# Graph network on one core: gather slots, index loads and table order of the attention edges

## What is computed

```python
def gatv2_layer(x, src, dst, Wl, bl, Wr, br, att, bias, n_nodes):
    C = att.shape[1]
    xl = (x @ Wl + bl).reshape(n_nodes, H, C)
    xr = (x @ Wr + br).reshape(n_nodes, H, C)
    e = jax.nn.leaky_relu(xl[src] + xr[dst], NEG_SLOPE)
    alpha = jnp.einsum('ehc,hc->eh', e, att)
    ...
    return out.mean(axis=1) + bias
```

## Time and profile before

| | us |
|---|---|
| median of 3 runs | 8165.79 (8153.4 to 8166.29) |
| the profiled execution's own time | 8135.08 |
| its span | 8133.5 |

### The profile page before, as it was taken

One profiled execution on the slowest core, in us unless ns is written; L12 is line 12 of the kernel. 1 busy time (PEld: TensorE's weight loads), 2 busy tenths in 40 slices (PEclk: granted clock), 3 DMA queues, 4 the chain that ended last, 5 costly groups with the idle time before them and its releaser, 6 DMA issues. The chain is left out here.

```text
span 8133.5 us, 102622 instructions
## 1 busy us (share of the span) xinstructions
PE 3894.0 (48%) x24731; PEld 3130.5 (38%) x24802; DVE 5407.7 (66%) x9588; ACT 2288.6 (28%) x3006; POOL 3503.5 (43%) x3810
## 2 busy tenths in 40 slices
PE   5777774000488826665362222223776222222476
PEld 2777773000388825565330000002763000001375
DVE  6777776968211146667437888885874888887686
ACT  5555553127122226566311111110001111111000
POOL 4766662001100067777515666661001666665100
PEclk9555555555699967877655555556975555555796
DMA  8899898955488723333336666663634666665462
GB/s 312 253 270 274 266 273 240 246 222 202 96 290 290 275 92 114 122 134 134 67 91 189 189 189 188 188 186 79 125 90 136 188 189 188 189 188 144 107 126 58
DMA packets 1551059, 1463.90 MB, mean 180 GB/s; under 512 B 1295757, under 2 KB 1343529, under 8 KB 1534460
## 3 DMA queue, kind: packets, MB, share of 16 engines
q1 hardware_dynamic: 976448, 824.48, 32.6%
q0 software_dynamic: 175712, 462.09, 20.9%
q10 hardware_dynamic: 398812, 176.37, 8.0%
HBM read 1080.92 MB, written 381.40 MB: 180 GB/s over the span
## 5 line engine op out<-in xcount | busy, mean ns | idle before, releaser
L2320 POOL DMA_INDIRECT rows_p<-node_rows,stage_i x1728 | 1638.0, 948 | 596.9 <-issue 482.7
L2356 PE MATMUL psZ<-parts_r,hot_t 126*128 x1728 | 629.6, 468 | 1859.8 <-DVE lz L2423 1720.0
L2356 PEld LDWEIGHTS psZ<-parts_r,hot_t 126*128 126x128 bf16 x1728 | 180.5, 104 | 2309.8 <-issue 2289.2
L2416 DVE TENSOR_TENSOR psZ<-psZ,rows_p 128x660 f32<-128x660 f32 x864 | 725.4, 847 | 476.1 <-DMA rows_p<-node_rows,stage_i 404.7
L257 POOL DMA_INDIRECT rows_s<-hpx,stage_i x784 | 740.5, 945 | 264.7 <-issue 240.7
L257 POOL DMA_INDIRECT both<-table,stage_i x784 | 740.5, 944 | 263.9 <-issue 239.7
L715 PE MATMUL psP<-window,pair_hot 128*128 x3136 | 715.8, 423 | 263.1 <-DVE pair_run L790 178.3
L715 PEld LDWEIGHTS psP<-window,pair_hot 128*128 128x128 f32 x3136 | 686.6, 331 | 295.8 <-issue 295.8
L2385 ACT ACTIVATE near<-locs,third 126x1536 bf16<-126x1536 bf16 x144 | 226.8, 1575 | 1923.4 <-DMA locs<-loc_rows 1923.3
L2423 DVE SCALAR_TENSOR_TENSOR lz<-psZ,att 128x660 f32<-128x660 f32 x864 | 722.9, 837 | 2.5
L2429 DVE TENSOR_REDUCE sc<-lz 128x10 f32<-128x660 f32 x864 | 711.8, 831 | 0.0
(11 more groups left out here) (523 smaller groups left out, 7527.7 us busy)
## 6 DMA issues: line engine op xcount, KB each, us to landing
tile<-adj SPq DMA_DIRECT2D x228, 781.2 KB, 4.6
xs<-x_src SPq DMA_DIRECT2D x648, 128.0 KB
x_src<-rows_p SPq DMA_DIRECT2D x144, 384.0 KB, 3.6
locs<-loc_rows SPq DMA_DIRECT2D x144, 378.0 KB
hpx<-stage ACTq DMA_DIRECT2D x25, 2048.0 KB, 7.5
pair_loc<-pair_locs SPq DMA_DIRECT2D x28, 1792.0 KB, 11.1
window<-hpx SPq DMA_DIRECT2D x196, 256.0 KB
dst_runs<-pair_run SPq DMA_DIRECT2D x28, 1792.0 KB
```

The costliest lines, as they stand in the source:

```text
L2320: pool.indirect_dma_start(rows[:, k, j, :], None, g.node_rows, bass.IndirectOffsetOnAxis(stage[:, k, j:j + 1], 0)).then_inc(got[k], 16)
L2356: last = pe.matmul(psZ[:, n % 4, j, 0:ZH], hot[:, k, col * CE:(col + 1) * CE], parts[:, bass.ds(at[col], 1), :].rearrange("p o c -> p (o c)"),
L2416: v.tensor_tensor(here, here, rows[:, k, m * G:(m + 1) * G, 0:ZH], ALU.add).then_inc(added, 1)
```

## The change

One function changes, `gat_edges`, in three ways.
- The ring of gathered rows has four slots of KS = 6 columns in place of two of twelve, with a semaphore of each kind per slot. The memory is the same. DVE waits for a slot at every third group (GS = 3) and marks it used there.
- POOL no longer copies indices. SP loads them from `srcT` into `stage`, a slot of six at a time: four loads ahead of the table stage, and one as soon as a slot's gathers have landed, ahead of the slot's store.
- The table stage does one source block and one target block per iteration, 25 times. The sum of both products is made by DVE (one more step) and not by PE. `parts` is loaded by one DMA from SP.

```diff
-    XK = (NB + 3) // 2
+    SLOTS = 4
+    KS = 2 * KC // SLOTS
+    GS = KS // G
     with phase(nc) as s:
-        stage = s.sb("stage_i", [P, 2, KC], i32)
+        stage = s.sb("stage_i", [P, SLOTS, KS], i32)
...
             def _(sp):
                 sp.dma_start(g.node_rows.rearrange("(p b) c -> p b c", b=NB)[:, :, ZH:TR], h[:, :, :]).then_inc(put, 16)
+                for k in range(SLOTS):
+                    sp.dma_start(stage[:, k, :], g.srcT[:, k * KS:(k + 1) * KS]).then_inc(index_in[k], 16)
...
-                def store(i, k):
-                    sp.wait_ge(got[k], i * (16 * KC) + 16 * KC)
-                    sp.dma_start(g.x_src.rearrange("(j p) c -> p j c", p=P)[:, bass.ds((i * 2 + k) * KC, KC), :],
+                def load_index(i, k):
+                    at = bass.ds(i * (SLOTS * KS) + k * KS, KS)
+                    sp.dma_start(stage[:, k, :], g.srcT[:, at]).then_inc(index_in[k], 16)
+
+                def store(i, k, last):
+                    sp.wait_ge(got[k], i * (16 * KS) + 16 * KS)
+                    if not last:
+                        load_index(i + 1, k)
+                    sp.dma_start(g.x_src.rearrange("(j p) c -> p j c", p=P)[:, bass.ds(i * (SLOTS * KS) + k * KS, KS), :],
                                  rows[:, k, :, ZH:TR]).then_inc(stored[k], 16)
...
                 with sp.Fori(0, NK // 2 - 1) as i:
                     load_locs(i, 1)
-                    store(i, 0)
+                    store(i, 0, False)
+                    store(i, 1, False)
                     load_locs(i + 1, 0)
-                    store(i, 1)
+                    store(i, 2, False)
+                    store(i, 3, False)
...
                 with pool.Fori(0, NK // 2) as i:
-                    c.begin(i, 2)
-                    for k in range(2):
-
+                    for k in range(SLOTS):
+                        pool.wait_ge(index_in[k], i * 16 + 16)
                         pool.wait_ge(used[k], i + 1)
                         pool.wait_ge(stored[k], i * 16 + 16)
-                        c.link(pool.tensor_copy(stage[:, k, :], g.srcT[:, bass.ds((i * 2 + k) * KC, KC)]))
                         pool.sem_inc(staged, 1)
-                        for j in range(KC):
+                        for j in range(KS):
...
+                    pe.transpose(psZ[0:D, 3, b % 2, 0:P], h[:, b, :], g.ident[:, :]).then_inc(n_turned, 1)
+                    pe.wait_ge(n_ready, b + 1)
...
+                    pe.matmul(psZ[:, 0, b % 2, 0:ZH], xT[:, b % 2, :], flat(g.wA[:, :, :]), start=True, stop=True)
+                    pe.matmul(psZ[:, 1, b % 2, 0:ZH], xT[:, b % 2, :], flat(g.wB[:, :, :]), start=True, stop=True).then_inc(n_made, 1)
...
-                    c.link(v.scalar_tensor_tensor(zs, psZ[:, 2, b % 2, 0:ZH], 0.0, att, ALU.max, ALU.mult))
+                    c.link(v.tensor_tensor(zs, tab[:, b % 2, :], psZ[:, 1, b % 2, 0:ZH], ALU.add))
                     c.mark(v.tensor_copy(x3[:, b % 2, 1, :], rest))
+                    c.link(v.scalar_tensor_tensor(zs, zs, 0.0, att, ALU.max, ALU.mult))
+                    c.mark(v.tensor_tensor(x3[:, b % 2, 2, :], rest, x3[:, b % 2, 1, :], ALU.subtract))
                     c.link(v.tensor_reduce(selfs[:, b, :], zs.rearrange("p (h c) -> p h c", h=H), X, ALU.add))
-                    c.link(v.tensor_tensor(x3[:, b % 2, 2, :], rest, x3[:, b % 2, 1, :], ALU.subtract))
...
-                            if m == 0:
-                                v.wait_ge(got[k], i * (16 * KC) + 16 * KC)
+                            slot, at = divmod(n, GS)
+                            if at == 0:
+                                v.wait_ge(got[slot], i * (16 * KS) + 16 * KS)
...
-                            if q % NG == NG - 1:
-                                v.sem_inc(used[q // NG], 1)
+                            if q % GS == GS - 1:
+                                v.sem_inc(used[q // GS], 1)
```

More of the change, by code:

```diff
@@ L2242, in gat_edges @@
         tab = s.sb("tab_rows", [P, 2, ZH])
-        xT, x3 = s.sb("xT", [D + 1, XK, P]), s.sb("x3", [P, 2, 3, ZH], bf16)
+        xT, x3 = s.sb("xT", [D + 1, 2, P]), s.sb("x3", [P, 2, 3, ZH], bf16)
         psZ = s.ps("psZ", [P, 4, G, 512])
         two = lambda name: [s.sem(f"{name}{k}") for k in range(2)]
[L2247 to L2250, removed]
+        locs_in, sent, tab_put = (two(n) for n in ("locs_in", "sent", "tab_put"))
+        slots = lambda name: [s.sem(f"{name}{k}") for k in range(SLOTS)]
+        used, stored, index_in = (slots(n) for n in ("slot_used", "stored", "index_in"))
+        got = [s.pool_sem(g, k) for k in range(SLOTS)]
+        dve_c, staged, put, parts_in, cleared = (
+            s.sem(n) for n in ("dve_c", "staged", "x_put", "parts_in", "cleared"))
         hot_made, made, added, prod, scored, neared = (s.sem(n) for n in ("hot_made", "made", "added", "prod", "scored", "neared"))
-        padded, n_turned, n_ready, n_made, n_tab, n_both, n_high, n_split = (
-            s.sem(n) for n in ("padded", "n_turned", "n_ready", "n_made", "n_tab", "n_both", "n_high", "n_split"))
-        sources = lambda b: range(2 * b, min(2 * b + 2, NB))
+        padded, n_turned, n_ready, n_made, n_tab, n_high, n_split = (
+            s.sem(n) for n in ("padded", "n_turned", "n_ready", "n_made", "n_tab", "n_high", "n_split"))
         grp = lambda i, n: i * (2 * NG) + (n + 1)
@@ L2292, in _ @@
                     load_locs(i, 1)
-                    store(i, 0)
+                    store(i, 0, False)
+                    store(i, 1, False)
                     load_locs(i + 1, 0)
-                    store(i, 1)
+                    store(i, 2, False)
+                    store(i, 3, False)
                 load_locs(NK // 2 - 1, 1)
-                store(NK // 2 - 1, 0)
-                store(NK // 2 - 1, 1)
-                for k in range(2):
+                for k in range(SLOTS):
+                    store(NK // 2 - 1, k, True)
+                for k in range(SLOTS):
                     sp.wait_ge(stored[k], 16 * (NK // 2) + 16)
@@ L2303, in _ @@
             def _(pool):
-                c = Chain(pool, pool_c)
                 pool.memset(parts[:, whole, :], 0.0).then_inc(cleared, 1)
-                for k in range(2):
+                for k in range(SLOTS):
                     pool.sem_inc(stored[k], 16)
@@ L2362, in _ @@
                 for b in range(NB):
[L2363 to L2370, removed]
-                    if b >= 2:
+                    act.wait_ge(n_turned, b + 1)
+                    if b >= 2:
+                        act.wait_ge(n_made, b - 1)
+                    act.activation(xT[0:D, b % 2, :], psZ[0:D, 3, b % 2, 0:P], ACT.Copy).then_inc(n_ready, 1)
+                    act.wait_ge(n_made, b + 1)
+                    if b >= 2:
+                        act.wait_ge(tab_put[b % 2], 16 * (b // 2))
                         act.wait_ge(n_split, b - 1)
+                    act.activation(tab[:, b % 2, :], psZ[:, 0, b % 2, 0:ZH], ACT.Copy).then_inc(n_tab, 1)
+                    if b >= 2:
                         act.wait_ge(sent[b % 2], 16 * (b // 2))
@@ L2376, in _ @@
                 act.sem_inc(hot_made, 2)
[L2377 to L2380, removed]
                 with act.Fori(0, NK // 2) as i:
@@ L2412, in turn @@
                             v.wait_ge(made, grp(i, n) + 2 * NG)
-                            if m == 0:
-                                v.wait_ge(got[k], i * (16 * KC) + 16 * KC)
+                            slot, at = divmod(n, GS)
+                            if at == 0:
+                                v.wait_ge(got[slot], i * (16 * KS) + 16 * KS)
                             here = psZ[:, n % 4, :, 0:ZH]
-                            v.tensor_tensor(here, here, rows[:, k, m * G:(m + 1) * G, 0:ZH], ALU.add).then_inc(added, 1)
+                            v.tensor_tensor(here, here, rows[:, slot, at * G:(at + 1) * G, 0:ZH], ALU.add).then_inc(added, 1)
                         if 1 <= n <= 2 * NG:
@@ L2433, in turn @@
                                 c.link(v.tensor_copy(g.sj[:, :, bass.ds((i * 2 + k) * KC, KC)], sc[:, k].rearrange("p j h -> p h j")))
+                for k in range(SLOTS):
+                    v.sem_inc(used[k], 1)
                 v.sem_inc(prod, 4)
```

36 lines of the change are left out of this document (12 added, 24 removed).

## The result

| | before | after |
|---|---|---|
| median of the runs, us | 8163.52 (8153.4 to 8166.29, 4 runs) | 7790.89 (7783.16 to 7800.02, 4 runs) |
| ratio, with 95% interval | | 0.9551 [0.954, 0.9562] |
| profiled execution, us | 8135.08 | 7795.55 |
| its span, us | 8133.5 | 7793.9 |
| layer 1: first gather, us behind the stage's start | 99.6 | 94.1 |

The change saves 372.6 us; the forecast was 326. The stage's start is the issue of the store of node features into `node_rows` (4120.38 before, 4143.95 after). The work ahead of it took 23.6 us longer in the profiled execution of after than in that of before, so stretches are compared from that start. In layer 1 the first add comes 32.3 us earlier and the loop is 151.5 us shorter, together 184. In layer 2 it is 31.9 and 151.3, together 183. Both layers make 367 of the 372.6.

The account below looks back on a forecast made before the run. POOL was taken to bound the loop, with gathers 1.25 us apart and 4 us per turn of waits and copies. Savings of 132 + 31 = 163 us per layer, 326 for two, gave 7809 profiled and 7840 as median; range 7780 to 7940.

Parts of the forecast that it names:

- What bounds the loop: Attention loop: POOL is the bound, with gathers 1.25 us apart and 4 us per turn of waits and copies.
- The turn of 30.5: Attention loop: a turn falls from 34.05 to 30.07 + 0.4 = 30.5 us; 35 turns make 1067.
- The rival of a 2.2 us branch back: Rival 3, POOL's loop end: the branch back costs 2.2 us once per turn, giving 7973; chance 0.09.
- 7.6 us until slot 0 is free: Loop start: with all slots full, POOL waits 7.6 us until slot 0 is free.
- The last landing: Loop end: 5.3 us from the last gather's end (5491.0) to the add behind it (5496.31).
- Block cycle: Table stage: each block takes 3.6 us, bound by the round trip between TensorE and ScalarE.
- the share of the gathers in its time: Hand-over: 24 gathers beside the load of `parts` add 16 us to its 23.7.
- Rival 1: Table stage: loop gains, tables don't, a wait on `sent` or `n_split` turning up in the cycle; 7902, chance 0.08.
- The 4282 end of the range: Hand-over: first add only at 4282, if `parts` on one queue instead of two takes 21 us longer.
- Slower by a longer pitch: Rival 5, loop: the gathers' pitch grows above 1.45 us; at 1.5, 86 us slower, 8250; chance 0.03.
- four waits for slots: Sign in the loop: VectorE idle about 2 us per turn, in four small waits.
- Sum: Both stages: 132 us less in the loop and 31 in the tables, 163 per layer, 326 for two.

Follow-up runs that it names:

- the run with the signal alone: Kernel before, with VectorE signalling slot 0 free ahead of its wait for slot 1's gathers; two slots, copies on POOL: 7974.37 against 8154.63 us, 0.9785.
- the tables-alone run: Kernel before with only the new table stage and one load of `parts`: 9283.75 against 9346.78 us, 0.9931, on a chip with stalls.
- the two-queue run: Changed kernel with `parts` loaded in halves by SP and ACT: 9414.66 us against 9487.47 for the kernel before, 0.9921, on a chip with stalls.
- slots and index loads alone: The change with before's table stage and two `parts` loads: 7865.01 against 8161.35 us, 0.9631; with stalls 9397.09 against 9346.78, 1.0056.
- copies back: Changed kernel with index copies on POOL again, against the kernel before, with stalls: 9408.42 against 9487.47 us, 0.9908; again 9412.7 against 9510.36, 0.9901.
- transposes ahead: Changed kernel, transposes one block ahead, first two `locs` loads before `parts`; against before, with stalls: 9409.22 against 9487.47 us, 0.9913; again 0.9908.

## Why the prediction was right, and where its sizes were off

**What bounds the loop: right.** POOL's wait was made by a signal behind an add that waits for the next slot. The run with the signal alone shows it: 2.6 us a turn of the 2.70 read.

**The turn of 30.5: a term was mis-sized.** I put 0.1 us on each slot's waits and 0.4 on a turn. They cost nothing: 840 gathers in 1050.0 us, borders and branches back included, against my 35 turns of 30.5, 1067. This is 17 us of the 19.5 a layer by which the loop came out better. The rival of a 2.2 us branch back falls with it. The wait rows of after suggest what hides them: the gathers behind a signal of VectorE show 0.3 us of idle time, and so do all the others.

**7.6 us until slot 0 is free: it was 4.0.** The signal needs add 2 to be done and stands in VectorE's order behind the issue of add 3, but it doesn't wait for add 3 to run: POOL goes on at 4287.65, and that add starts at 4288.16. I had counted a whole slot. The last landing (5.7 against 5.3) and the last three groups (9.5) were as read.

**Overlooked: the first count-up of the slots moved.** Before, VectorE gave POOL its slots ahead of the table stage; now it does so behind its last table step. The first gather of after waits on just that (93.69 us, for line 2436), about 1.5 us behind the table (an estimate: in the tables-alone run, where the signal stands early, the table has landed 92.5 us behind the stage's start, and here the gather starts at 94.1). It costs nothing in the end, since POOL stands 19.92 us with full slots anyway.

**The tables: right in each step.** Block cycle 3.59 us for 3.6; `parts` 48.4 us earlier behind the stage's start for 47; the share of the gathers in its time 40.2 - 23.7 = 16.5 for 16; the first add 32.3 us earlier for 31. Rival 1, a late wait on `sent` in the cycle, did not come: `tab` to `tab` is steady at 3.59 to the last block. The 4282 end of the range, 21 us more for one queue, did not come either: after itself has one queue, and the two-queue run is at most 3 us faster there.

**Slower by a longer pitch: no.** VectorE works 93% of a turn beside POOL (280.66 of 300.5 us from 4574.5), the DMA engines 81% (forecast 76%), and the gather stays at 946 ns. VectorE's 2 us of idle time a turn came as written, but not as four waits for slots: layer 1 has 23 waits for gathers in all, 28.5 us together.

**Sum.** 184 us a layer against 163. Of the 46 us by which the forecast missed, the loop makes 39 (17 a layer by the waits of the slots), the tables 3. The other 5 us are outside these stretches; what they are is not shown, and the runs of after alone spread over 17 us.

## What to carry to other kernels

Read where a "buffer free" signal stands in the program order of the engine that gives it: behind an instruction that waits for the next buffer, it makes the filling engine stand until that buffer has landed, once a turn here, and moving that one signal gave 180 us of saving where four slots and SP's index loads together gave 296. In this loop, waits on semaphores that were already satisfied cost nothing beside the 0.30 us that stand ahead of every gather, so four smaller slots were free. A table that must be complete before gathers may start, and a load that follows it, should be ordered so that the load and the first gathers share the DMA engines, and the price of it is the gathers' own engine time, 16.5 us here.

## What the chip showed that was not expected

On three of the six chips that these measurements met, the engines slow down or stand still together for some us, and this takes back what a denser loop gains. Windows of slots and index loads alone on such a chip, then of after (columns as above):

```profile
5600.00:5900.00 300.00, 76.65 (x210) 21.85 (x210) 247.83 (x334) 53.46 (x35) 197.26 (x208) 0.50 0.71 184
```

```profile
4574.50:4875.00 300.50, 88.63 (x244) 25.37 (x244) 280.66 (x384) 61.16 (x40) 227.30 (x241) 0.50 0.81 214
```

The same loop issues 208 gathers in 300 us instead of 241, with the same durations and the same granted clock of 0.50 (1.2 GHz). A stretch of the first one's timeline:

```profile
5866.06 0.95 POOL L2332 DMA_INDIRECT rows_p<-node_rows,stage_i  x1 [0.31 <-issue]
...
5867.40 0.85 DVE L2428 TENSOR_TENSOR psZ<-psZ,rows_p 128x660 f32<-128x660 f32 x1 [0.55 <-issue]
5868.81 0.85 DVE L2435 SCALAR_TENSOR_TENSOR lz<-psZ,att 128x660 f32<-128x660 f32 x1 [0.56 <-issue]
...
5872.46 0.95 POOL L2332 DMA_INDIRECT rows_p<-node_rows,stage_i  x1 [5.46 <-issue]
```

POOL stands 5.46 us without a releaser, and VectorE's steps meanwhile are 1.4 us apart, where they follow each other by about 0.75 elsewhere. Most of what such a chip adds to the kernel lies ahead of the attention layers: in the tables-alone run their stage starts at 5299.7 instead of 4120.4. The loop of before, with 34.1 us a turn and a DMA share of 0.69 in the tables-alone run, shows none of it on the same chip, and every version made for less comes to about 35: the mean of layer 1's turns lies between 34.8 and 35.5 us by POOL's gathers in all eight such runs, whether the turns without a stall take 30, 31.4 or 32.9. There the whole change is worth little: the three variants nearest to it (copies back, two queues, transposes ahead) stand at 0.990 to 0.992 of before, 73 to 98 us less, not much more than the 63 of the tables alone. After itself was not run on such a chip. What in the chip does this is open: for the stalls themselves the traces name no instruction or DMA of the kernel as releaser, and neither the slots, the copies nor the signal changed it. A lesson for measuring follows: a saving read on one chip need not hold on the next, and the turns without a stall still show a kernel's own pace.
